# TensorE's order in an attention stage: a pacing rule replaced by a plan over three engines, and a shorter lead

## What is computed

```python
x = L0_attn_x                                   # 1 x 4096 x 256
xn = _layernorm(x)
s = _L0_attn_ref(xn, ...)                       # transformer block: 16 heads of 16, causal
g = _silu(_L0_ffn_ref(xn, ...))                 # mixture of 8 experts with a shared fallback
x = x + s * g
...
scores = jnp.einsum('bhqd,bhkd->bhqk', q, k) / math.sqrt(hd)
scores = jnp.where(causal[None, None], -jnp.inf, scores)
attn = jax.nn.softmax(scores, axis=-1)
attn_out = jnp.einsum('bhqk,bhkd->bhqd', attn, v)
```

## Time and profile before

| | |
|---|---|
| median of three runs | 2322.44 us (2320.7 to 2323.6) |
| the profiled execution: span, first to last instruction | 2321.9 us; no other time is recorded for it |
| TensorE matmul busy | 2217.7 us (96%) |
| VectorE busy | 1960.4 us (84%) |
| ScalarE busy | 1454.6 us (63%) |
| mean granted TensorE clock | 0.969 of 2.4 GHz |
| attention stage | 358.7 to 1896 us |

### The profile page before, as it was taken

The page is one execution under the profiler, slowest core; times in us unless marked ns, Lnnn a source line. Parts: engine busy times, 40 slices in busy tenths (PEclk is TensorE's granted clock), DMA queues, the critical chain, the costliest instruction groups (busy, mean ns, idle before and its releaser), DMA issues. The chain is left out here.

```text
span 2321.9 us, 48508 instructions
## 1 busy us (share of the span) xinstructions
PE 2217.7 (96%) x18612; PEld 1338.0 (58%) x18612; DVE 1960.4 (84%) x3755; ACT 1454.6 (63%) x1778; POOL 214.7 (9%) x287
## 2 busy tenths in 40 slices
PE   3999987999999999999999999999999989999998
PEld 2889883444444444444444444444444438998998
DVE  7888977889999988999999989988888817777887
ACT  3534320277777777777777777778777775555443
POOL 3110101010021300000000000000000000000544
PEclk9999995699999999999999999999999999999999
DMA  6232337012101111110001130000210015453222
GB/s 157 95 126 106 111 127 124 6 34 68 33 13 44 52 45 35 34 45 12 12 12 35 34 103 12 12 22 1 32 22 4 4 47 193 151 153 98 85 95 81
DMA packets 138295, 143.68 MB, mean 62 GB/s; under 512 B 36168, under 2 KB 101320, under 8 KB 137976
## 3 DMA queue, kind: packets, MB, share of 16 engines
q1 hardware_dynamic: 132624, 129.68, 19.6%
q0 software_dynamic: 3072, 8.39, 1.1%
q10 hardware_dynamic: 2432, 3.28, 0.5%
HBM read 88.17 MB, written 51.02 MB: 60 GB/s over the span
## 5 line engine op out<-in xcount | busy, mean ns | idle before, releaser
L1155 DVE TENSOR_REDUCE attn_MX<-psB 128x1 f32<-128x512 f32 (+3 forms) x2176 | 1332.2, 670 | 158.9 <-PE psB L969 103.2
L1128 ACT ACTIVATE attn_PB<-psB 128x1024 f32<-128x1024 f32 (+3 forms) x1152 | 1075.3, 953 | 381.4 <-PE psB L1023 313.0
L969 PE MATMUL psB<-KS,attn_QS 52*128 52x512 f32 (+3 forms) x1152 | 327.8, 453 | 26.4 <-DMA KS<-picking_rows 17.7
L1045 PE MATMUL psB<-attn_PB,V 128*32 128x256 f32 (+4 forms) x4016 | 332.8, 403 | 1.5
L1045 PE MATMUL psB<-attn_PB,attn_V 128*32 128x256 f32 (+5 forms) x3560 | 322.4, 434 | 1.6 <-ACT attn_PB L1128 0.6
L969 PE MATMUL psB<-attn_KS,attn_QS 52*128 52x512 f32 (+3 forms) x1152 | 282.9, 408 | 2.7 <-DVE attn_MX L1155 1.4
L1023 PE MATMUL psB<-attn_QS,KS 52*128 52x512 f32 (+3 forms) x1152 | 279.7, 469 | 0.1
L1023 PE MATMUL psB<-attn_QS,attn_KS 52*128 52x512 f32 (+3 forms) x1152 | 273.9, 461 | 5.4 <-ACT attn_PB L1128 3.4
L969 PEld LDWEIGHTS psB<-KS,attn_QS 52*128 52x128 f32 x1152 | 188.2, 199 | 97.4 <-DVE attn_MX L1155 67.5
L1023 PEld LDWEIGHTS psB<-attn_QS,attn_KS 52*128 52x128 f32 x1152 | 110.9, 184 | 229.0 <-issue 109.8
L1023 PEld LDWEIGHTS psB<-attn_QS,KS 52*128 52x128 f32 x1152 | 111.5, 184 | 213.9 <-issue 140.6
(11 more groups left out here) (239 smaller groups left out, 3096.1 us busy)
## 6 DMA issues: line engine op xcount, KB each, us to landing
W<-in_w SPq DMA_DIRECT2D x18, 1024.0 KB, 5.6
qk_parts<-proj_PT SPq DMA_DIRECT2D x32, 512.0 KB, 2.8
attn_QS<-qk_parts SPq DMA_DIRECT2D x192, 64.0 KB
v_rows<-proj_VA SPq DMA_DIRECT2D x32, 256.0 KB, 2.0
attn_KS<-qk_parts SPq DMA_DIRECT2D x96, 64.0 KB, 2.6
KS<-qk_parts SPq DMA_DIRECT2D x90, 64.0 KB, 3.0
XN<-in_x SPq DMA_DIRECT2D x8, 512.0 KB, 9.3
rows_by_place<-proj_ZR SPq DMA_DIRECT2D x32, 128.0 KB, 2.4
```

The source lines that it names most:

```text
L969: mm = nc.tensor.matmul(ps[:, bank, at * width:(at + 1) * width], QS[rows, i % 4, b, j * P:(j + 1) * P], KS[w][rows, b, kc * CH:kc * CH + ...
L1045: mm = nc.tensor.matmul(ps[32 * h:32 * (h + 1), PV, cols], V[w][:, kb, 32 * h:32 * (h + 1)], PB[:, u % RING, h, cols], start=(k == 0 and f ...
L1128: nc.scalar.activation(PB[:, u % RING, 2 * pair:2 * pair + 2, r * P:CH], ps[:, 2 * (s % 2):2 * (s % 2) + 2, r * P:CH], ACT.Exp, scale=HD * ...
L1155: nc.vector.tensor_reduce(MX[:, m % 4, first:first + 2 * n - 1:2, kc], ps[:, MB + off % 3, 0:n * w].rearrange("p (h n) -> p h n", h=n), AX ...
```

## The change

`max_pass_pace` keeps its taut path, but starts from a lead given to it, and counts time by columns alone. What it returns is now only a goal for a new planner, `plan_products`. The planner walks through the 1152 pairs of scores in order. For each pair it tries how many jobs to issue behind it (0 to 3), then how many product halves (0 to 2), then how many more jobs (0 to 2, only behind a half). It carries for each candidate the times at which TensorE's two row groups, VectorE and ScalarE would be done, by constants for each operation, and keeps up to `KEPT_STATES` = 2 candidates for each count of jobs and halves. The count of jobs may differ from the goal by `SPREAD` = 4, and products may stay up to `LAG` = 4 halves behind. The best path at the end is the plan. TensorE's loop writes it out. The lead is now the first step's jobs and `LEAD` = 16 more, with the first rows made behind `ROWS_LEAD` = 8 of them. ScalarE's copy of a step's sums moves to behind the pair behind which the plan has issued the step's last product.

No operation's shape changes, other than that products are cut in halves at other places. VectorE, GpSimd and SyncE keep their own orders.

```diff
-def max_pass_pace(steps, units, jobs, j_base):
+def max_pass_pace(steps, units, jobs, j_base, lead):
...
-    when = [0.0] + list(itertools.accumulate(UNIT + (1 - UNIT) * (TPC - units[i][k][1]) / TPC for i, k in order))
-    least, most = [end(AHEAD)], [end(AHEAD)]
+    when = [0.0] + list(itertools.accumulate((TPC - units[i][k][1]) / TPC for i, k in order))
+    least, most = [lead], [lead]
...
+LEAD, ROWS_LEAD = 16, 8
+LAG, SPREAD, KEPT_STATES = 4, 4, 2
+SWITCH, WEIGHTS, NARROW_WEIGHTS, MASK_WEIGHTS = 96, 107, 27, 14
+COLUMN, TWO_PASS_COLUMN = 0.4415, 1.667
+PE_TO, FROM_DVE, FROM_ACT = 205, 134, 158
+REDUCE, REDUCE_COLUMN, FINISH = 68, 1.0417, 693
+ACTIVATE, ACTIVATE_COLUMN, ROWS_MOVE = 80, 0.82, 2500
+def plan_products(steps, units, jobs, j_base, starts, rows_at):
...
+    pace = max_pass_pace(steps, units, jobs, j_base, j_base[1] + LEAD)
...
+    goal = [op_at(pace[i][k]) for i, k, _ in pairs]
+    high = [min(goal[n] + SPREAD, op_at(j_base[min(i + 1 + AHEAD, LS)])) for n, (i, _, _) in enumerate(pairs)]
+    low = [goal[n] - SPREAD for n in range(len(pairs))]
...
+    def stream(x, mode, groups, time, load, ready):
+        at = x[ISSUED] = max(x[ISSUED], ready)
+        if mode != x[MODE]:
+            at, x[MODE] = max(at, max(x[ENDED:ENDED + 2]) + SWITCH), mode
+        begin = max([at + load] + [x[BEGUN + g] + load for g in groups] + [x[ENDED + g] for g in groups])
+        for g in groups:
+            x[BEGUN + g], x[ENDED + g] = begin, begin + time
+        return begin + time
...
+        x[ROWS] = x[EXPD + 1] + ROWS_MOVE
...
+        for back in front:
+            x = score(back[0], n)
+            for before in range(4):
+                x = job(x) if before and x else x
+                y = x
+                for count in range(3):
+                    y = half(y, n) if count and y else y
+                    z = y
+                    for after in range(3 if count else 1):
+                        z = job(z) if after and z else z
+                        if z:
+                            keep(z, back, (before, count, after))
...
-                for m in range(AHEAD):
-                    for n in range(len(jobs[m])):
-                        max_jobs(m, n)
-                        if m == 1 and n == 7:
-                            max_rows(0, 0, None, 1)
...
+                before_rows = sum(first < j_base[1] + ROWS_LEAD for first, _, _ in starts)
+                ask(before_rows)
+                max_rows(0, 0, None, 1)
+                ask(sum(first < j_base[1] + LEAD for first, _, _ in starts) - before_rows)
...
+                for n, (before, halves, after) in enumerate(plan):
+                    (i, k), pair = flat[n // 2], n % 2
+                    scores(i, k, pair)
+                    if pair == 1 and k == rows_at(i) and i + 1 < LS:
+                        max_rows(i + 1, s_rows(i), s_rows(i) - 1, i + 2)
+                    ask(before)
+                    weigh_halves(halves)
+                    ask(after)
...
-                        if k == 0 and i > 0:
-                            sums(i - 1)
...
+                            if n in sums_behind:
+                                sums(sums_behind[n])
+                            n += 1
```

More of the change, by code:

```diff
@@ L729, in max_pass_pace @@
         most.append(end(i + 1 + AHEAD))
-    path, at = [work[end(AHEAD)]], 0
+    path, at = [work[lead]], 0
     while at < len(order):
@@ L744, in max_pass_pace @@
         at = turn
-    upto, count = [[] for _ in range(LS)], end(AHEAD)
+    upto, count = [[] for _ in range(LS)], lead
     for (i, k), goal, lo, hi in zip(order, path[1:], least[1:], most[1:]):
@@ L772, in attend @@
     j_base = [sum(len(j) for j in jobs[:i]) for i in range(LS + 1)]
-    ahead = [(m, n) for m in range(LS) for n in range(len(jobs[m]))]
-    upto = max_pass_pace(steps, units, jobs, j_base)
     RING = 3
     rows_at = lambda i: len(units[i]) - 3
+    starts = [(j_base[m] + n, m, job) for m in range(LS) for n, job in enumerate(jobs[m])
+              if n % 2 == 0 or job[0] is None or job[2] < steps[m][1]]
+    plan = plan_products(steps, units, jobs, j_base, starts, rows_at)
+    made = list(itertools.accumulate(halves for _, halves, _ in plan))
+    sums_behind = {next((n for n, count in enumerate(made) if count >= 2 * u_base[i + 1]), None): i for i in range(LS)}
     s_of = lambda i, k, pair: s_base[i] + 2 * k + pair + (1 if rows_at(i) < k and i + 1 < LS else 0)
@@ L980, in hide_later_keys, with max_jobs @@
                     return nc.tensor.matmul(out, later_qk[half][rows, :], hide[rows, 0:n, :], start=False, stop=(half == 1))
[L982 to L987, removed]
+                def max_jobs(off, i, job):
+                    j, _, kc = job
+                    if j is None or kc < steps[i][1]:
+                        max_job(i, off, job).then_inc(maxed, 1)
                         return
[L989 to L992, removed]
+                    both = jobs[i][off - j_base[i]:off - j_base[i] + 2]
                     for n, job in enumerate(both):
@@ L1077, in _ @@
[L1077 to L1096, removed]
@@ L1097, in _ @@
-                weigh(*behind, 0, CH)
+                asked = 0
+                def ask(count):
+                    nonlocal asked
+                    for _ in range(count):
+                        max_jobs(*starts[asked])
+                        asked += 1
+                before_rows = sum(first < j_base[1] + ROWS_LEAD for first, _, _ in starts)
+                ask(before_rows)
+                max_rows(0, 0, None, 1)
+                ask(sum(first < j_base[1] + LEAD for first, _, _ in starts) - before_rows)
@@ new lines, in _, with weigh_halves @@
+                flat = [(i, k) for i in range(LS) for k in range(len(units[i]))]
+                weighed = 0
+                def weigh_halves(count):
+                    nonlocal weighed
+                    upto = weighed + count
+                    while weighed < upto:
+                        i, k = flat[weighed // 2]
+                        mid = (units[i][k][1] * P + CH) // 2
+                        both = weighed % 2 == 0 and weighed + 2 <= upto
+                        weigh(i, k, mid if weighed % 2 else 0, CH if both or weighed % 2 else mid)
+                        weighed += 2 if both else 1
@@ L1099, in _ @@
+                weigh_halves(2 * len(flat) - weighed)
             @block.scalar
@@ L1118, in _ @@
                 rows(0, 0, 1)
+                n = 0
                 for i in range(LS):
```

119 lines of the change are left out of this document (110 added, 9 removed).

## The result

The changed kernel takes **2311.0 us** in the median of six runs (2298.4 to 2316.6). The kernel before, run beside it, takes 2324.1 (2320.7 to 2328.7). The ratio is 0.9932, with a 95% interval from 0.9912 to 0.9952. It is faster, by 13 us between the medians and by 0.68% (11 to 20 us) by the ratio, where -70 was forecast, and 2311 lies outside the range of 2216 to 2304.

What follows compares the result with a forecast made beforehand. Attention was taken as bound by TensorE's work plus about 121 us of waits, from arrangement, not capacity. Terms -37 + 7 + 11 - 51 = -70 from the span of 2321.9 gave 2252 us, range 2216 to 2304.

Steps and rivals of the forecast that it cites:

- The lead, -37: Start of attention: with fewer jobs ahead, the first score moves from 444.0 to about 407.3, saving 37 us.
- What comes back, +7 and +11: Jobs now inside the stage cost TensorE 7 us; reductions setting the pace in the first four steps cost 11.
- TensorE's own work there is 174: First four steps, new order: TensorE needs 174 us against 185 of reductions, so reductions set the pace, +11 us.
- a start at 1.2 GHz and the tail together: Waits said to remain at the slow-clock start and in the ScalarE-paced tail: some 15 us.
- The waits, -51: Attention stage: TensorE's waits on other engines fall from about 121 to 70 us by better arrangement, saving 51.
- the 65 waits of products should go: Products standing up to three pairs behind their exponential should lose their 65 waits on it; reason given for -51 us.
- Plain stretches: TensorE stretches of one pair and two jobs: mean to fall from 0.737 to near 0.70 us, a sign of being right.
- Waits stay: Rival: the attention's waits are not removed, only the lead and its price remain; 2303 us, 2285 to 2318, chance 0.15.
- Starts in program order: Rival: 93 stretches of lower job, pair, upper job each cost 0.225 us more; 2276 us, chance 0.07.
- Rows too late, and then a slow clock: Rival: late rows at step boundaries, then slow clock, 4.4 us each; 2388 us if all 31 struck, chance 0.06.

Runs made afterwards that it cites:

- r3: The changed kernel with four more unread 512-column matmuls behind each of the last eight lead jobs: 2301.5 us, ratio 0.9906 to the kernel before.
- s4: The changed kernel with SyncE sending the next step's rows ahead of the sums' stores, and `LEAD` at 44: 2279.9 us, ratio 0.9781 to the kernel before.
- t3: The changed kernel with SyncE sending the next step's rows ahead of the sums' stores, and `LEAD` at 30: ratio 0.9815 to the kernel before.
- r2: The changed kernel with the long lead of the kernel before (`LEAD` 76 instead of 16), planned from there: ratio 0.9887 to the kernel before.
- r1: The kernel before, its pacing rule and loop kept, with the changed kernel's short lead and nothing of the plan: 2320.8 us.
- r4: The changed kernel with SyncE sending the next step's maximum rows ahead of the wait for the last step's sums and their stores: ratio 0.9879 to the kernel before.
- t2: The changed kernel with whole products in the first 24 score groups and SyncE's rows sent first: five runs from 2270.0 to 2293.4 us.
- s1: The changed kernel with the long lead (`LEAD` 76) and SyncE's rows sent ahead of the sums: 2287.8 us, ratio 0.9807 to the kernel before.
- s2: The changed kernel with product halves of the first 24 score groups joined to whole 512-column products: 2306.8 us.

## Why the prediction was wrong

**The lead, -37: right in itself.** The first score came at 406.3 where 407.3 was forecast, bound by the rows' landing as much as by the jobs.

**What comes back, +7 and +11: mis-sized, and for the wrong reason.** Together with the lead these made -19 by the end of step 3, and the work of VectorE up to there (192 us) leaves room for no more than 24. But the step "TensorE's own work there is 174" took it at full clock. The prediction allowed some 15 us for a start at 1.2 GHz and the tail together. In the trace of before the clock rose 8 us behind the first score; now it stayed low for 63. TensorE, not VectorE, was the bound there, the excess over the least in steps 0 to 3 went from 17 to 44 us, and step 4's rows came 5 us later instead of 19 earlier. r3 shows the half clock to be the bound (with the clock up VectorE is full again), and s4 and t3 that a lead of 30 or 44 keeps 12 us of the gain. Why the clock stays low stays open.

**The waits, -51: this is the step that failed.** From step 4 on they fell by 20 us, not 51. Some 10 more went back to late rows: with the rows first the excess there is 67.5 instead of 77.8. No trace of this plan shows more of the 51 than these 31 taken away. In the terms of the table, 115 us above the least were to become some 75 (51 less, 11 more) and became 122. Of these 47 us, 31 lie from step 4 on and 16 in the first four steps; the stage is 53 us longer than forecast. The reason given, that "the 65 waits of products should go", is refuted by the list: they became 115, and waits of jobs on reductions went from 160 to 419. VectorE's idle before reductions fell to 119.7 us, from 135.7, where about 90 was foretold. The plan took slack from VectorE's side and put its queue in TensorE's way. Plain stretches did come near the forecast 0.70: 234 of "pair, two jobs" have a mean of 0.69 and 57 and 50 with both jobs ahead of the pair 0.74 and 0.75, some 0.71 together, so the forecast erred mostly in the stretches that are not plain. The largest excess stands in stretches of diagonal jobs with masks, as the one at 567.4 with eight of them, 3.2 us above its least.

**Waits stay (0.15).** 2311 lies in its range of 2285 to 2318, its 2303 is the nearest of the prices, and its stage of 1469 us was met with 1470.7. That is luck: the plan is worth 26 us with the long lead (r2, 0.9887 of 2324), so the waits did not all stay, and the short lead, which that rival had at 19 us less, costs some 10 with the plan (r2 against after) and wins 6 without it (r1).

**Starts in program order (0.07): refuted.** In the timeline of after, a job for the lower row group ahead of the pair and one for the upper behind it (which group is whose follows from the order, not from the rows):

```profile
862.44 0.50 PE L1131 MATMUL psB<-attn_KS,attn_QS 52*128 52x512 f32 x1
862.44 0.72 PE L1181 MATMUL psB<-attn_QS,attn_KS 52*128 52x512 f32 x2
862.78 0.39 PE L1131 MATMUL psB<-attn_KS,attn_QS 52*128 52x512 f32 x1
863.10 0.64 PE L1203 MATMUL psB<-attn_PB,attn_V 128*32 128x256 f32 x8
```

It takes 0.66 us, and 90 such stretches have a median of 0.67; 0.88 was foretold if starts were in program order. The rule of the Trainium skill ("TensorE: Matmul & The Clock Gate", Part 3) does not hold for matmuls on different row groups here.

**Rows too late, and then a slow clock (0.06).** It struck three boundaries and not 31, and so lay inside my range by the text. The mechanism and its price for one boundary were right: 6.3 us of waits, and 12 us by r4, 4 us each, against 4.4. What the prediction named as the cause, the sums' store ahead of the rows in SyncE's queue, is what r4 undoes.

**The range and the chances.** The high side of the range took both the lead's gain and the full clock as given. A clock that stays low behind the first score had no rival of its own, though the earlier trace rows had its price.

## What to carry to other kernels

Before a lead or prologue is cut, add up what the engine that it keeps busy must do until the next point of balance: here VectorE's 193 us up to step 4, in the order as paced, capped the gain at 24 us of the 37, however early the first score. When a planner moves the last use of a buffer later, look at what stands in a DMA queue behind that use: sending the urgent transfer first was worth as much as the whole change. And tell a clock loss from a wait by the same instruction's duration in two places (1.08 against 0.64 us) before more is tuned.

## What the chip showed that I had not expected

The granted clock stayed at 0.50 to 0.52 for 64 us while the profile shows TensorE busy for 63.3 of them, with the same shapes of matmuls that ran at full clock from 469 on. The Trainium skill ("TensorE: Matmul & The Clock Gate", Part 1) has the gate set by how busy the array has been recently. The busy time that the profile shows does not tell when it rises, as these 64 us show. The same part of the Trainium skill tells of a kernel in which the array idles for short moments between groups of matmuls so often that its clock goes up and down. In after the clock stayed low instead; in t2 it did go up and down (up at 419, down at 429, up at 463), but no run here shows that such moments are the cause. The same engine, given four more matmuls behind each of eight jobs ahead of the score, ran at 0.99 for the next 34 us, and then fell as well. Falls occur at waits of 1.3 us (before) to 2.7 us, and at places where no wait is over 1 us: s1's at 737 stands behind one of 0.97 us for an exponential, and lasts 20 us.

The same kernel's runs differ with their mean granted clock: after's six go from 2298.4 at 0.965 to 2316.6 at 0.955, t2's five from 2270.0 at 0.979 to 2293.4 at 0.965. That is 16 to 18 us for each 0.01. Read at one clock, by a straight line through each kernel's runs, at 0.970 before stands at 2324, r1 at 2325, after at 2289, r2 and r4 at 2287, t2 at 2285, s4 at 2282 and t3 at 2281. r3 and s2 stand at 2294 to 2295. So the plan's kernels are some 29 to 43 us below before at an equal clock, and by this reading after's mean of 0.959 against 0.969 is what separates -13 from -35. It is a reading of the runs and no experiment: a wait that lowers the clock is also lost time.
